# Low-rank part in four PSUM banks of its own, added by VectorE, with TensorE's work of a batch in blocks

## The chip, the cores and the metric

The kernel runs on one core of a Trainium2 chip. A core has TensorE (PE, matrix products), VectorE (DVE), ScalarE (ACT), GpSimd (POOL) and SyncE (SP), which here only issues DMAs. Each engine runs its own instruction list; semaphores order them. The metric is the device time of one execution in microseconds (us), taken as the median of several runs.

## The reference

There are 64 batches of x, each 128 channels by 2048 time steps, in fp32. Each batch b draws one of 16 square matrices W (128 by 128) and one of 64 low-rank adapters (B: 16 by 2048, A: 2048 by 16):

```python
    x = x + _L0_cond_ref(x, L0_cond_weights, itok_B_0_15)   # einsum('bct,bcd->bdt', x, W[cond])
    x = x + _L1_cond_ref(x, L1_cond_A, L1_cond_B, itok_B_4_50)
    # Bx = einsum('bni,bri->bnr', x, B[ids]);  out = einsum('bnr,bor->bno', Bx, A[ids])
    return x
```

With M = W + identity the first line is f = Mᵀx. The second adds the low-rank part: z = f · Bᵀ (a 16-vector for each channel), then A · z.

## The kernel before

A batch is held turned, time on the partitions: 16 chunks of 128 time steps, four chunks make a unit, and a unit of f fills one PSUM bank (128 by 512 fp32). There are 8 banks. For each batch:

- GpSimd picks M (`pick_m`, line 184) and splits A into a rounded part and a rest (`round_a`, `rest_of_a`, lines 188 and 193). VectorE turns 32 by 32 blocks of that (`turn_a`, line 290), GpSimd copies it to `at` (`place_at`, line 198).
- TensorE makes f unit by unit: `mix_unit`, line 349, four products of x (stationary) with M into `f_bank` or `f_last`.
- ScalarE copies each unit of f to SBUF, tile `ft` (`copy_unit`, line 249).
- TensorE sums z from `ft` and B: `sum_z`, line 362, 16 products whose stationary side is 16 columns wide, into one half of `zg_bank`. VectorE copies z (`join_z`, line 295), TensorE repeats it over the partitions (`spread_z`, line 372, into the other half of the same bank), VectorE splits it into g_hi and g_lo (`split_g`, lines 300 and 302).
- TensorE adds the low-rank part (`add_low_rank`, line 384): 32 products of 32 rows, accumulated onto f in the very banks that hold f. So f's banks stay taken from the mix to the end of the low rank.
- ScalarE copies units 3 and 1 to `x_out` and VectorE units 0 and 2 (`evacuate`, lines 253 and 283); SP stores `x_out` (line 157).

Units 0 to 2 of f have two banks each (for even and odd batches), unit 3 has one, `f_last`, for all batches; with `zg_bank` these are the eight. The order on each engine is written out by hand in the `turn` functions, four batches to a loop pass. On TensorE it interleaves: low rank of b; z of b+1 for three units; mix of unit 3 of b+1; mix of unit 0 of b+2; z of unit 3 of b+1; mix of unit 1; spread; mix of unit 2.

Of the kernel before, what the change touches and what calls it, by code (L numbers as in the profile page):

```python
# [11 lines left out]
P = 128  # L12
# [17 lines left out]
LEAVES = (3, 0, 1, 2)  # L30
BY_ACT, BY_DVE = LEAVES[0::2], LEAVES[1::2]
# [9 lines left out]
def exists(b, last):  # L41

    return not (last and b >= BODY)


def cond_lora_residual(nc, x, cond_ids, adapter_ids, weights, lora, out):
    with ExitStack() as ctx:  # L47
# [23 lines left out]
        ft = [[sbuf(f"ft{i}{u}", [P, UNIT]) for u in range(UNITS)] for i in range(2)]  # L71
# [36 lines left out]
        act_evacuated = sem("act_evacuated")  # L108
        dve_evacuated = sem("dve_evacuated")
# [7 lines left out]
        def _(sp):  # L117
# [26 lines left out]
            def turn(q, last):  # L144
                for k in range(BODY):
                    b = BODY * q + k
                    if not last:
                        sp.wait_ge(f_made, UNITS * (b + 1))
                        load_x(k, b + BODY)
                        adapter = adapter_of(b + BODY)  # L150
                        sp.wait_ge(z_done, b + 1)
                        sp.wait_ge(a_split, b + 1)
                        load_ab(k, adapter)
                    if not (last and k >= BODY - 2):
                        sp.wait_ge(act_evacuated, len(BY_ACT) * (b + 1))
                        sp.wait_ge(dve_evacuated, len(BY_DVE) * (b + 1))
                        sp.dma_start(out[b], x_out[k][:]).then_inc(stored[k], 16)
# [5 lines left out]
            for b in (BATCHES - 2, BATCHES - 1):  # L163
                for i, u in enumerate(LEAVES):
                    cols = slice(UNIT * u, UNIT * (u + 1))
                    if u in BY_ACT:
                        sp.wait_ge(act_evacuated, len(BY_ACT) * b + i // 2 + 1)
                    else:
                        sp.wait_ge(dve_evacuated, len(BY_DVE) * b + i // 2 + 1)
                    sp.dma_start(out[b, :, cols], x_out[b % BODY][:, cols]).then_inc(stored[b % BODY], 16)  # L170
# [4 lines left out]
        def _(pool):  # L175
# [29 lines left out]
            for k in range(2):  # L205
                pool.wait_ge(ab_loaded[k], 16)
                round_a(k)
                rest_of_a(k, k)
            pool.wait_ge(a_turned, 1)
            place_at(0)  # L210
# [3 lines left out]
            def turn(q, last):  # L214
                for k in range(BODY):
                    b = BODY * q + k
                    if exists(k + 3, last):
                        if live(UNITS * b):
                            pool.wait_ge(f_made, UNITS * b)
                        if exists(k + 2, last):  # L220
                            pool.wait_ge(a_turned, b + 1)
                            pool.wait_ge(ab_loaded[(k + 2) % BODY], 16 * (q + (k + 2) // BODY + 1))
                        pick_m((k + 3) % BODY, b + 3)
                    if exists(k + 2, last):
                        if not exists(k + 3, last):
                            pool.wait_ge(a_turned, b + 1)
                            pool.wait_ge(ab_loaded[(k + 2) % BODY], 16 * TURNS)
                        round_a((k + 2) % BODY)
                        pool.wait_ge(a_turned, b + 2)
                        if live(b):  # L230
                            pool.wait_ge(low_done, b)
                        rest_of_a((k + 2) % BODY, b + 2)
                        place_at(k + 1)
# [11 lines left out]
        def _(act):  # L245
            def copy_unit(k, u, b):

                act.wait_ge(f_made, UNITS * b + u + 1)
                nc.scalar.copy(ft[k % 2][u][:], f_bank[k % 2][u][:]).then_inc(copied, 1)  # L249

            def evacuate(k, u):

                nc.scalar.copy(x_out[k][:, UNIT * u:UNIT * (u + 1)], f_bank[k % 2][u][:]).then_inc(act_evacuated, 1)  # L253

            for u in range(UNITS):
                copy_unit(0, u, 0)
            for u in range(UNITS - 1):
                copy_unit(1, u, 1)

            def turn(q, last):  # L260
                for k in range(BODY):
                    b = BODY * q + k
                    if live(q):
                        act.wait_ge(stored[k], 16 * q)
                    act.wait_ge(low_done, b + 1)
                    for u in BY_ACT:
                        evacuate(k, u)
                    if exists(k + 1, last):
                        copy_unit(k + 1, UNITS - 1, b + 1)
                    if exists(k + 2, last):  # L270
                        for u in range(UNITS - 1):
                            copy_unit(k + 2, u, b + 2)

            turn(0, False)
            with act.Fori(1, TURNS - 1) as q:
                turn(q, False)
            turn(TURNS - 1, True)

        @block.vector
        def _(dve):  # L280
            def evacuate(k, u):

                nc.vector.tensor_copy(x_out[k][:, UNIT * u:UNIT * (u + 1)], f_bank[k % 2][u][:]).then_inc(dve_evacuated, 1)  # L283
# [26 lines left out]
            join_z(0)  # L310
            split_g(0)

            def turn(q, last):
                for k in range(BODY):
                    b = BODY * q + k
                    if live(q):
                        dve.wait_ge(stored[k], 16 * q)
                    dve.wait_ge(low_done, b + 1)
                    for u in BY_DVE:
                        evacuate(k, u)  # L320
                    if exists(k + 1, last):
                        turn_a(k + 1, b + 1)
                        join_z(b + 1)
                        split_g(b + 1)
# [7 lines left out]
        def _(pe):  # L332
            def mix_unit(k, u, b, turns):
# [8 lines left out]
                before = b - 1 if u == UNITS - 1 else b - 2  # L342
                if live(before + 1):
                    if u in BY_ACT:
                        pe.wait_ge(act_evacuated, len(BY_ACT) * before + BY_ACT.index(u) + 1)
                    else:
                        pe.wait_ge(dve_evacuated, len(BY_DVE) * before + BY_DVE.index(u) + 1)
                for c in range(IN_UNIT):
                    last = nc.tensor.matmul(f_bank[k % 2][u][:, P * c:P * (c + 1)],  # L349
# [4 lines left out]
            def sum_z(k, units, b, turns):  # L354

                if units[0] == 0:
                    pe.wait_ge(ab_loaded[k % BODY], 16 * turns)
                for u in units:
                    pe.wait_ge(copied, UNITS * b + u + 1)
                    for c in range(IN_UNIT):  # L360
                        first = RANK * (IN_UNIT * u + c)
                        last = nc.tensor.matmul(z_ps[TILE * c:TILE * c + RANK, :],  # L362
                                                ab_in[k % BODY][:, first:first + RANK],
                                                ft[k % 2][u][:, P * c:P * (c + 1)],
                                                start=(u == 0), stop=(u == UNITS - 1))
                if units[-1] == UNITS - 1:
                    last.then_inc(z_done, 1)
# [7 lines left out]
            def add_low_rank(k, b):  # L375

                pe.wait_ge(at_made, b + 1)
                for made, part in ((g_rounded, g_hi), (g_split, g_lo)):
                    pe.wait_ge(made, b + 1)
                    for c in range(IN_UNIT):  # L380
                        for u in range(UNITS):
                            rows = slice(BLOCK * u, BLOCK * (u + 1))
                            js = slice(c * (P // BLOCK), (c + 1) * (P // BLOCK))
                            last = nc.tensor.matmul(f_bank[k % 2][u][:, P * c:P * (c + 1)],  # L384
                                                    at[k % 2][rows, js, :].rearrange("m j i -> m (j i)"), part[rows, :],
                                                    start=False, stop=(part is g_lo and c == IN_UNIT - 1),
# [7 lines left out]
            mix_unit(1, 0, 1, 1)  # L394
            sum_z(0, (0, 1, 2, 3), 0, 1)
            mix_unit(1, 1, 1, 1)
            spread_z(0)
            mix_unit(1, 2, 1, 1)
# [61 lines left out]
```

## Time and profile before

| | |
|---|---|
| median of 3 runs | 427.61 us (427.53 to 429.12) |
| profiled execution, its own time | 432.05 us |
| profiled execution, span | 430.3 us |
| busy, share of the span: PE, PEld | 96%, 84% |
| busy: DVE, ACT, POOL | 42%, 51%, 31% |
| granted TensorE clock, mean | 0.991 of full speed |
| DMA | 152.37 MB, mean 354 GB/s |

PE are TensorE's matmuls, PEld its weight loads, which run beside matmuls. A busy PE doesn't mean PE at its peak: matmuls are pipelined, their ends are modelled, and the distance from one start to the next tells what a step costs. Each fp32 product is recorded twice, so 16 products are 32 records; the narrower low-rank products (fp32r) are recorded once.

### The profile page before, as it was taken

To read this page: it belongs to the slowest core of one execution; us is meant where nothing else is said; L and a number is where in the kernel's file an instruction comes from. 1 tells how busy PE (TensorE), PEld (TensorE's weight loads), DVE (VectorE), ACT (ScalarE), POOL (GpSimd) and SP (SyncE) were. 2 spreads that over 40 slices of the span, in tenths; PEclk is the share of its full clock that TensorE was granted. 3 is DMA by queue.
4 is the path that set the end of the run, shared out by engine and by line. 5 is a ranking of instruction groups with operands and counts; after the bars stand their busy time and mean duration, and the time that the engine had idled before them with its cause. 6 is when DMAs were issued, how large, how long until landed. Compare 5 with 4: busy or idle time off the path is not lost.

```text
span 430.3 us, 16398 instructions
## 1 busy us (share of the span) xinstructions
PE 412.4 (96%) x6272; PEld 363.2 (84%) x6272; DVE 179.2 (42%) x386; ACT 219.9 (51%) x385; POOL 131.9 (31%) x263
## 2 busy tenths in 40 slices
PE   2999998999999999999999999999999999999993
PEld 2988886888888888888888888888888888888882
DVE  1334433444344344344344444444434434434433
ACT  1455553455555555555555555555555555555551
POOL 1343231332332331332332332233233133233220
PEclk9999998999999999999999999999999999999998
DMA  7999997899999999999999999999999999999645
GB/s 234 340 404 422 403 377 308 312 375 361 372 383 358 366 382 360 357 393 367 362 380 368 360 379 373 366 363 383 360 359 393 360 364 381 358 363 389 258 178 195
DMA packets 29777, 152.37 MB, mean 354 GB/s; under 512 B 3268, under 2 KB 3524, under 8 KB 13764
## 3 DMA queue, kind: packets, MB, share of 16 engines
q1 hardware_dynamic: 29764, 152.19, 95.2%
q8 instruction: 9, 0.15, 0.1%
q14 instruction: 4, 0.03, 0.0%
HBM read 85.07 MB, written 67.11 MB: 354 GB/s over the span
## 4 chain that ended last, share of the span: by engine, by line
PE 96%; DMA 1%; issue 1%; SPq 1%; DVE 0%; DVEq 0%; ACT 0%; POOL 0%; POOLq 0%
PE f_bank L349 44%; PE zg_bank L362 17%; PE f_last L349 17%; PE f_bank L384 15%; PE zg_bank L372 3%; DMA w_first<-in_L_cond_weights 1%; PE f_last L384 0%; SPq L131 0%; DVE x_out L283 0%; SPq L134 0%; DVEq L47 0%; ACT ft L249 0%; POOL m_sel L204 0%; SPq L127 0%; DVE z_t L295 0%
## 5 line engine op out<-in xcount | busy, mean ns | idle before, releaser
L349 PE MATMUL f_bank<-m_sel,x_in 128*128 128x128 f32 x1536 | 212.3, 282 | 8.2 <-POOL m_sel L204 8.2
L349 PEld LDWEIGHTS f_bank<-m_sel,x_in 128*128 128x128 f32 x1536 | 189.7, 195 | 21.7 <-issue 21.7
L249 ACT COPY ft<-f_bank 128x512 f32<-128x512 f32 x192 | 112.4, 586 | 118.2 <-PE f_bank L349 118.2
L193 POOL TENSOR_TENSOR a_hl<-ab_in,a_hl 128x256 fp32r<-128x256 f32 x64 | 46.6, 728 | 258.4 <-DVE at_turn L290 258.1
L283 DVE COPY x_out<-f_bank 128x512 f32<-128x512 f32 x128 | 82.4, 686 | 88.3 <-PE f_last L384 88.3
L362 PE MATMUL zg_bank<-ft,ab_in 128*16 128x128 f32 x2048 | 80.8, 276 | 0.7 <-ACT ft L249 0.7
L349 PEld LDWEIGHTS f_last<-m_sel,x_in 128*128 128x128 f32 x512 | 62.3, 192 | 17.2 <-ACT x_out L253 15.0
L349 PE MATMUL f_last<-m_sel,x_in 128*128 128x128 f32 x512 | 74.7, 289 | 2.1 <-issue 2.1
L249 ACT COPY ft<-f_last 128x512 f32<-128x512 f32 x64 | 37.5, 585 | 51.3 <-PE f_last L349 51.3
L362 PEld LDWEIGHTS zg_bank<-ft,ab_in 128*16 128x16 f32 x2048 | 44.8, 96 | 13.1 <-ACT ft L249 0.9
L253 ACT COPY x_out<-f_last 128x512 f32<-128x512 f32 x64 | 37.5, 585 | 35.3 <-PE f_last L384 35.3
L295 DVE COPY z_t<-zg_bank 128x128 f32<-128x128 f32 x64 | 18.6, 291 | 80.2 <-PE zg_bank L362 80.2
L290 DVE STREAM_TRANSPOSE at_turn<-a_hl 128x512 f32<-128x512 f32 x64 | 44.9, 701 | 11.3 <-POOL a_hl L193 11.3
L300 DVE CAST g_hi<-zg_bank 128x128 fp32r<-128x128 f32 x64 | 18.6, 291 | 63.1 <-PE zg_bank L372 63.1
L384 PE MATMUL f_bank<-g_hi,at 32*128 32x128 f32 x768 | 42.5, 283 | 0.5 <-DVE g_hi L300 0.5
L384 PE MATMUL f_last<-g_hi,at 32*128 32x128 f32 x256 | 42.1, 283 | 0.0
L198 POOL CAST at<-at_turn 128x512 fp32r<-128x512 f32 x64 | 39.0, 610 | 5.1 <-DVE at_turn L290 5.1
L384 PEld LDWEIGHTS f_bank<-g_hi,at 32*128 32x128 f32 x768 | 33.5, 185 | 8.2 <-issue 0.6
L384 PE MATMUL f_bank<-g_lo,at 32*128 32x128 f32 x768 | 39.2, 270 | 0.0
L384 PE MATMUL f_last<-g_lo,at 32*128 32x128 f32 x256 | 38.8, 270 | 0.0
L253 ACT COPY x_out<-f_bank 128x512 f32<-128x512 f32 x64 | 37.9, 592 | 0.0
L384 PEld LDWEIGHTS f_bank<-g_lo,at 32*128 32x128 f32 x768 | 33.9, 187 | 0.0
(18 smaller groups left out, 187.2 us busy)
## 6 DMA issues: line engine op xcount, KB each, us to landing
x_in<-in_x SPq DMA_DIRECT2D x63, 1024.0 KB, 7.0
out<-x_out SPq DMA_DIRECT2D x62, 1024.0 KB, 5.0
ab_in<-in_lora SPq DMA_DIRECT2D x64, 256.0 KB, 5.8
out<-x_out SPq DMA_DIRECT2D x8, 256.0 KB, 3.2
x_in<-in_x SPq DMA_DIRECT2D x4, 256.0 KB, 4.0
w_first<-in_L_cond_weights SPq DMA_DIRECT2D x2, 64.0 KB, 4.2
ids<-in_itok_B SPq DMA_DIRECT2D x2, 0.2 KB
w_all<-in_L_cond_weights SPq DMA_DIRECT2D x1, 0.5 KB, 8.6
```

The lines of the kernel that those rows point to most:

```text
L193: nc.gpsimd.tensor_tensor(a_hl[k % 2][:, :, RANK:HL], raw_a(k), a_hl[k % 2][:, :, 0:RANK], ALU.subtract).then_inc(a_split, 1)
L198: nc.gpsimd.tensor_copy(at[k % 2][:], at_turn[:]).then_inc(at_made, 1)
L249: nc.scalar.copy(ft[k % 2][u][:], f_bank[k % 2][u][:]).then_inc(copied, 1)
L253: nc.scalar.copy(x_out[k][:, UNIT * u:UNIT * (u + 1)], f_bank[k % 2][u][:]).then_inc(act_evacuated, 1)
L283: nc.vector.tensor_copy(x_out[k][:, UNIT * u:UNIT * (u + 1)], f_bank[k % 2][u][:]).then_inc(dve_evacuated, 1)
L290: nc.vector.transpose(at_turn[:], a_hl[k % 2][:].bitcast(F32)).then_inc(a_turned, 1)
L295: nc.vector.tensor_copy(z_t[:], z_ps).then_inc(z_joined, 1)
L300: nc.vector.tensor_copy(g_hi[:], g_ps).then_inc(g_rounded, 1)
L349: last = nc.tensor.matmul(f_bank[k % 2][u][:, P * c:P * (c + 1)], x_in[k][:, UNIT * u + P * c:UNIT * u + P * (c + 1)], m_sel[k][:], start= ...
L362: last = nc.tensor.matmul(z_ps[TILE * c:TILE * c + RANK, :], ab_in[k % BODY][:, first:first + RANK], ft[k % 2][u][:, P * c:P * (c + 1)], s ...
L372: nc.tensor.matmul(g_ps, spread[:].rearrange("k n r -> k (n r)"), z_t[:], start=True, stop=True).then_inc(g_done, 1)
L384: last = nc.tensor.matmul(f_bank[k % 2][u][:, P * c:P * (c + 1)], at[k % 2][rows, js, :].rearrange("m j i -> m (j i)"), part[rows, :], sta ...
```

## The change

The low-rank part no longer accumulates onto f. It has four banks of its own, `low_bank`, and f gets three, `f_bank0` to `f_bank2`; unit 3 goes to bank 0 again (`BANK_OF`). ScalarE copies f to `ft` and does nothing else; `ft` has four buffers, one for each batch of a pass. VectorE writes all of `x_out`: x_out = low_bank + ft, four adds a batch. TensorE does a batch's work in blocks, and the low rank comes one batch later. SP issues the A and B load and the store later against the x load; GpSimd does A one batch ahead in place of two.

```diff
-LEAVES = (3, 0, 1, 2)
-BY_ACT, BY_DVE = LEAVES[0::2], LEAVES[1::2]
+BANK_OF = (0, 1, 2, 0)
...
-        ft = [[sbuf(f"ft{i}{u}", [P, UNIT]) for u in range(UNITS)] for i in range(2)]
+        ft = [[sbuf(f"ft{i}{u}", [P, UNIT]) for u in range(UNITS)] for i in range(BODY)]
...
-        f_last = psum("f_last")
-        f_bank = [[psum(f"f_bank{i}{u}") for u in range(UNITS - 1)] + [f_last] for i in range(2)]
+        f_bank = [psum(f"f_bank{i}") for i in range(max(BANK_OF) + 1)]
+        low_bank = [psum(f"low_bank{u}") for u in range(UNITS)]
... SP, in turn(q, last)
-                        adapter = adapter_of(b + BODY)
-                        sp.wait_ge(z_done, b + 1)
-                        sp.wait_ge(a_split, b + 1)
-                        load_ab(k, adapter)
-                    if not (last and k >= BODY - 2):
-                        sp.wait_ge(act_evacuated, len(BY_ACT) * (b + 1))
-                        sp.wait_ge(dve_evacuated, len(BY_DVE) * (b + 1))
-                        sp.dma_start(out[b], x_out[k][:]).then_inc(stored[k], 16)
+                    if begun(b - 1) and exists(k + BODY - 1, last):
+                        adapter = adapter_of(b + BODY - 1)
+                        sp.wait_ge(z_done, b)
+                        sp.wait_ge(a_split, b)
+                        load_ab((k - 1) % BODY, adapter)
+                    if begun(b - 2):
+                        sp.wait_ge(added, UNITS * (b - 1))
+                        sp.dma_start(out[b - 2], x_out[(k - 2) % BODY][:]).then_inc(stored[(k - 2) % BODY], 16)
... ScalarE
+                    if live(q):
+                        act.wait_ge(added, UNITS * (b - BODY + 1))
+                    for u in range(UNITS):
+                        copy_unit(k, u, b)
... VectorE
+            def add_unit(k, u):
+
+                nc.vector.tensor_tensor(x_out[k][:, UNIT * u:UNIT * (u + 1)], low_bank[u][:], ft[k][u][:],
+                                        ALU.add).then_inc(added, 1)
+
+            def add_batch(k, b, turns):
+
+                if live(turns):
+                    dve.wait_ge(stored[k], 16 * turns)
+                dve.wait_ge(low_done, b + 1)
+                for u in range(UNITS):
+                    add_unit(k, u)
... TensorE
-                before = b - 1 if u == UNITS - 1 else b - 2
+                left = UNITS * (b if u == UNITS - 1 else b - 1) + (1 if u == UNITS - 1 else UNITS if u == 0 else u + 1)
+                if live(left):
+                    pe.wait_ge(copied, left)
...
+            def sum_z(k, b, turns):
+
+                pe.wait_ge(ab_loaded[k], 16 * turns)
+                pe.wait_ge(copied, UNITS * (b + 1))
+                if live(b):
+                    pe.wait_ge(g_split, b)
...
             def add_low_rank(k, b):
 
                 pe.wait_ge(at_made, b + 1)
+                if live(b):
+                    pe.wait_ge(added, UNITS * b)
...
-                            last = nc.tensor.matmul(f_bank[k % 2][u][:, P * c:P * (c + 1)],
+                            last = nc.tensor.matmul(low_bank[u][:, P * c:P * (c + 1)],
...
+                        for u in range(UNITS):
+                            mix_unit(k + 1, u, b + 1, q + (k + 1) // BODY + 1)
+                    sum_z(k, b, q + 1)
+                    if begun(b - 1):
+                        add_low_rank((k - 1) % BODY, b - 1)
+                    spread_z(b)
```

TensorE, one batch of the kernel before, in the first pass of four batches, with the low rank's last rows ahead of it (zg_bank is written by z with ft and ab_in, and by the spread with z_t):

```order
L384 MATMUL f_bank<-g_lo,at 128x128 x3
L384 MATMUL f_last<-g_lo,at 128x128
L362 MATMUL zg_bank<-ft,ab_in 16x128 x12
L349 MATMUL f_last<-m_sel,x_in 128x128 x4
L349 MATMUL f_bank<-m_sel,x_in 128x128 x4
L362 MATMUL zg_bank<-ft,ab_in 16x128 x4
L349 MATMUL f_bank<-m_sel,x_in 128x128 x4
L372 MATMUL zg_bank<-z_t,spread 128x128
L349 MATMUL f_bank<-m_sel,x_in 128x128 x4
L384 MATMUL f_bank<-g_hi,at 128x128 x3
```

TensorE, one batch of the changed kernel, in the first pass, with the spread ahead of it (the low rank is that of the batch before; f's units 0 and 3 share a bank):

```order
L354 MATMUL zg_bank<-z_t,spread 128x128
L331 MATMUL f_bank<-m_sel,x_in 128x128 x16
L345 MATMUL zg_bank<-ft,ab_in 16x128 x16
L368 MATMUL low_bank<-g_hi,at 128x128 x16
L368 MATMUL low_bank<-g_lo,at 128x128 x16
L354 MATMUL zg_bank<-z_t,spread 128x128
```

The four mixes have moved together, z is in one piece behind them, and the low rank stands between z and the spread.

VectorE, one batch of the first pass before:

```order
L283 COPY x_out<-f_bank 128x512 x2
L290 STREAM_TRANSPOSE at_turn<-a_hl 128x512
L295 COPY z_t<-zg_bank 128x128
L300 CAST g_hi<-zg_bank 128x128
L302 TENSOR_TENSOR g_lo<-zg_bank,g_hi 128x128
```

VectorE, one batch of the changed first pass (x_out and the adds are those of the batch before, z_t and g_hi of this one):

```order
L283 COPY z_t<-zg_bank 128x128
L262 TENSOR_TENSOR x_out<-low_bank,ft 128x512 x4
L288 CAST g_hi<-zg_bank 128x128
L290 TENSOR_TENSOR g_lo<-zg_bank,g_hi 128x128
L278 STREAM_TRANSPOSE at_turn<-a_hl 128x512
```

Four adds now stand between z_t and g_hi, where the two stood next to each other with two copies behind the split.

## Rows read from the trace of the kernel before

**Rows 1.** The page: busy time and share of each engine; the chain that ended last.

```profile
PE 412.4 (96%) x6272; PEld 363.2 (84%) x6272; DVE 179.2 (42%) x386; ACT 219.9 (51%) x385; POOL 131.9 (31%) x263
...
PE 96%; DMA 1%; issue 1%; SPq 1%; DVE 0%; DVEq 0%; ACT 0%; POOL 0%; POOLq 0%
```

**Rows 2.** Timeline, weight loads of a batch: start, length, engine, line, tiles, count [idle before].

```profile
200.77 0.19 PEld L384 LDWEIGHTS f_bank<-g_hi,at 32*128 32x128 f32 x3
...
201.81 0.57 PEld L362 LDWEIGHTS zg_bank<-ft,ab_in 128*16 128x16 f32 x24
...
202.59 0.97 PEld L349 LDWEIGHTS f_last<-m_sel,x_in 128*128 128x128 f32 x8 [0.21 <-ACT x_out L253]
...
203.48 0.97 PEld L349 LDWEIGHTS f_bank<-m_sel,x_in 128*128 128x128 f32 x8
...
204.57 0.13 PEld L362 LDWEIGHTS zg_bank<-ft,ab_in 128*16 128x16 f32 x8
...
204.92 0.97 PEld L349 LDWEIGHTS f_bank<-m_sel,x_in 128*128 128x128 f32 x8 [0.21 <-issue]
...
205.80 0.30 PEld L372 LDWEIGHTS zg_bank<-z_t,spread 128*128 128x128 f32 x2
...
206.03 0.97 PEld L349 LDWEIGHTS f_bank<-m_sel,x_in 128*128 128x128 f32 x8
...
207.12 0.19 PEld L384 LDWEIGHTS f_bank<-g_hi,at 32*128 32x128 f32 x3
```

**Rows 3.** Timeline at the start: z of batch 0, its z_t, M of batch 2.

```profile
15.18 0.79 PEld L362 LDWEIGHTS zg_bank<-ft,ab_in 128*16 128x16 f32 x32
...
16.18 0.97 PEld L349 LDWEIGHTS f_bank<-m_sel,x_in 128*128 128x128 f32 x8 [0.21 <-issue]
...
16.31 0.29 DVE L295 COPY z_t<-zg_bank 128x128 f32<-128x128 f32 x1 [1.73 <-PE zg_bank L362]
...
18.13 0.46 POOL L184 TENSOR_TENSOR m_sel<-w_all,ident 128x128 f32<-128x128 f32 x1 [2.59 <-DMA w_all<-in_L_cond_weights]
```

**Rows 4.** Timeline of VectorE in the same batch.

```profile
199.98 0.29 DVE L300 CAST g_hi<-zg_bank 128x128 fp32r<-128x128 f32 x1 [0.99 <-PE zg_bank L372]
200.31 0.29 DVE L302 TENSOR_TENSOR g_lo<-zg_bank,g_hi 128x128 fp32r<-128x128 f32 x1
201.93 1.29 DVE L283 COPY x_out<-f_bank 128x512 f32<-128x512 f32 x2 [1.33 <-PE f_last L384]
203.14 0.70 DVE L290 STREAM_TRANSPOSE at_turn<-a_hl 128x512 f32<-128x512 f32 x1
```

**Rows 5.** The page, DMA issues: KB each, us from issue to landing.

```profile
x_in<-in_x SPq DMA_DIRECT2D x63, 1024.0 KB, 7.0
```

**Rows 6.** Stretches: length, busy us (instructions) by engine, PEclk, DMA share, GB/s.

```profile
30.00:40.00 10.00, 10.00 (x171) 8.86 (x170) 4.76 (x11) 5.66 (x10) 2.04 (x4) 1.00 1.01 419
40.00:50.00 10.00, 10.00 (x136) 8.93 (x135) 4.17 (x10) 5.17 (x9) 4.16 (x8) 1.00 1.02 413
...
100.00:150.00 50.00, 50.00 (x760) 43.97 (x752) 22.10 (x48) 26.75 (x48) 16.38 (x32) 1.00 1.01 370
```

**Rows 7.** Timeline at the end: last z_t, spread, g_hi, low rank, copies.

```profile
421.88 0.29 DVE L295 COPY z_t<-zg_bank 128x128 f32<-128x128 f32 x1 [1.03 <-PE zg_bank L362]
422.23 0.30 PEld L372 LDWEIGHTS zg_bank<-z_t,spread 128*128 128x128 f32 x2 [0.70 <-DVE z_t L295]
...
422.75 0.29 DVE L300 CAST g_hi<-zg_bank 128x128 fp32r<-128x128 f32 x1 [0.58 <-PE zg_bank L372]
...
423.16 0.22 PEld L384 LDWEIGHTS f_bank<-g_hi,at 32*128 32x128 f32 x3 [0.64 <-issue]
...
424.42 1.29 DVE L283 COPY x_out<-f_bank 128x512 f32<-128x512 f32 x2 [1.05 <-PE f_last L384]
```

**Rows 8.** Timeline: the spreads on either side of the longest batch.

```profile
61.61 0.30 PEld L372 LDWEIGHTS zg_bank<-z_t,spread 128*128 128x128 f32 x2
...
71.85 0.30 PEld L372 LDWEIGHTS zg_bank<-z_t,spread 128*128 128x128 f32 x2
```

More of the change, by code:

```diff
@@ L38, in live, with exists, begun @@
     return not (isinstance(count, int) and count <= 0)
-def exists(b, last):
-    return not (last and b >= BODY)
+def exists(k, last):
+    return not (last and k >= BODY)
+def begun(b):
+    return not (isinstance(b, int) and b < 0)
 def cond_lora_residual(nc, x, cond_ids, adapter_ids, weights, lora, out):
@@ L204, in _ @@
                 nc.gpsimd.tensor_tensor(m_sel[k][:], w_first[k][:], ident[:], ALU.add).then_inc(m_picked, 1)
[L205 to L210, printed above, removed]
+            pool.wait_ge(ab_loaded[0], 16)
+            round_a(0)
+            rest_of_a(0, 0)
             pool.wait_ge(w_in, 16)
@@ L248, in copy_unit @@
                 act.wait_ge(f_made, UNITS * b + u + 1)
[L249 to L258, printed above, removed]
+                nc.scalar.copy(ft[k][u][:], f_bank[BANK_OF[u]][:]).then_inc(copied, 1)
             def turn(q, last):
@@ L263, in turn @@
                     if live(q):
[L264 to L272, printed above, removed]
+                        act.wait_ge(added, UNITS * (b - BODY + 1))
+                    for u in range(UNITS):
+                        copy_unit(k, u, b)
             turn(0, False)
-            with act.Fori(1, TURNS - 1) as q:
+            with act.Fori(1, TURNS) as q:
                 turn(q, False)
-            turn(TURNS - 1, True)
         @block.vector
         def _(dve):
-            def evacuate(k, u):
-                nc.vector.tensor_copy(x_out[k][:, UNIT * u:UNIT * (u + 1)], f_bank[k % 2][u][:]).then_inc(dve_evacuated, 1)
+            def add_unit(k, u):
[7 more added lines that the diff above has]
+                    add_unit(k, u)
             def turn_a(k, b):
@@ L352, in mix_unit @@
                 last.then_inc(f_made, 1)
[L354 to L359, printed above, removed]
+            def sum_z(k, b, turns):
+                pe.wait_ge(ab_loaded[k], 16 * turns)
+                pe.wait_ge(copied, UNITS * (b + 1))
+                if live(b):
+                    pe.wait_ge(g_split, b)
+                for u in range(UNITS):
                     for c in range(IN_UNIT):
@@ L383, in add_low_rank @@
                             js = slice(c * (P // BLOCK), (c + 1) * (P // BLOCK))
-                            last = nc.tensor.matmul(f_bank[k % 2][u][:, P * c:P * (c + 1)],
+                            last = nc.tensor.matmul(low_bank[u][:, P * c:P * (c + 1)],
                                                     at[k % 2][rows, js, :].rearrange("m j i -> m (j i)"), part[rows, :],
-                                                    start=False, stop=(part is g_lo and c == IN_UNIT - 1),
+                                                    start=(part is g_hi and c == 0), stop=(part is g_lo and c == IN_UNIT - 1),
                                                     skip_group_check=True)
```

84 lines of the change are left out of this document (27 added, 57 removed).

## The prediction, made before the changed kernel was run

> **What bounds the kernel now.** I read the page's engine shares and its chain first [rows 1]: TensorE is busy for 96% of the span and is 96% of the chain that ended last; VectorE is busy for 42%, ScalarE 51%, GpSimd 31%. So only what TensorE spends or waits for counts, and I need its batch in pieces. Since matmuls overlap, I read the starts of the weight loads (PEld), one start to the next.
>
> One batch, from low rank to low rank, is 207.12 − 200.77 = 6.35 us; most are 0.04 longer, with the wait on x_out behind z at 0.25; 6.38 on average. Its pieces [rows 2]:
> - low rank, 32 loads: 201.81 − 200.77 = 1.04
> - z of three units, 24 loads: 202.59 − 201.81 = 0.78
> - mix of f_last (8 loads: each fp32 matmul appears twice): 0.89
> - mix of a unit, with z behind it: 204.57 − 203.48 = 1.09
> - z of the fourth unit, 8 loads: 0.35
> - mix, with the spread behind it: 0.88
> - spread: 0.23
> - mix, with the low rank behind it: 1.09
>
> Two things stand in this list. First, 8 loads of a mix take 0.89 where another full-array product follows and 1.09 where z or the low rank follows: 0.20 for changing kind. The same step lies behind z: between its last load and the first of the mix PEld is idle for 0.21, once put down to ScalarE and once to "issue", with nothing to wait for. At the start 32 z loads in one piece take 16.18 − 15.18 = 1.00 [rows 3], while 24 and 8 apart take 0.78 + 0.35 = 1.13. So a change of kind costs about 0.2 at either side, waits or not. Second, two mixes in a row cost nothing extra although the second one's unit has its own wait: waits that are met are free.
>
> There are five such changes in a batch now: low to z, z to mix, mix to z, z to mix, mix to low.
>
> **The change on TensorE.** The same 98 matmul records a batch (6272 / 64 [rows 1]), in another order: four mixes, z, low rank of the batch before, spread. Three changes of kind are left: mix to z, z to low, low to spread.
> - mixes: 3 × 0.89 + 1.09 = 3.76 (before 0.89 + 1.09 + 0.88 + 1.09 = 3.95)
> - z in one block: 1.00 (before 1.13)
> - low rank: 1.04, spread: 0.23 as before
> - sum 6.03, against 6.38: 0.35 less in each batch.
>
> Two of these changes, z to low and low to spread, are not in the trace. From below each could cost nothing (0.4 less a batch), from above twice the 0.2 that others cost (0.4 more). Four that it does show cost 0.20 to 0.21, in both directions between full-array and narrow products; the fifth, low to z, narrow to narrow, lies inside the 1.04. I take the same for the two new ones: they are inside the 1.00 and the 1.04.
>
> **What the new waits ask for.** I count from T, the load of a batch's spread, which follows the low rank of the batch before.
> - VectorE starts its x_out work about 0.17 behind T: 201.93 against 201.81 here [rows 2, 4], up to 0.19 in other batches. Two 512-wide copies and the start of the next instruction are 203.14 − 201.93 = 1.21, so 0.605 each. The adds are four tensor_tensor from PSUM and SBUF. No such 512-wide row exists. From below: the copy's 0.605. From above: four times the 128-wide tensor_tensor out of PSUM, g_lo's 4 × 0.29 = 1.16 [rows 4]. I take 0.605, for g_lo takes the same 0.29 as the g_hi cast of the same width, so the second operand adds nothing there. Four adds: 2.42.
> - g_hi 0.33 and g_lo 0.29 behind them: done at T + 0.17 + 2.42 + 0.62 = T + 3.21, seen by TensorE at about T + 3.35.
> - The next z waits for g_split (it shares zg_bank), and would start at T + 0.23 + 3.76 = T + 3.99. The wait is met with 0.6 to spare. It comes out late once an add takes over 0.76.
> - turn_a (0.70) ends at T + 3.95, before z is done at T + 5.0; then z_t takes 0.29, and the spread is due at T + 6.03. Met. Queued behind join_z on VectorE are the adds, which can't start before T + 6.2 anyway.
> - GpSimd works 131.9 / 64 = 2.1 us a batch [rows 1] between a turn_a and the next; its at copy is due about 6 us after it is done. Met.
> - ScalarE has four copies instead of six: 219.9 / 385 = 0.57 each, 2.3 of 6.03. f_bank0 is filled twice a batch: the fourth mix starts 2.67 after the first, whose bank is filled 1.2 after its first load and copied 0.6 later. Met.
> - The DMA queue (SP) now waits for added of the batch two back, between the loads. x of batch b + 4 is issued when mix b is done and is needed 4 × 6.03 − 3.76 = 20 us later; a load lands in 7.0 [rows 5]. Stores have as much room. Met.
>
> **Transfers.** A batch moves 2.36 MB (two of 1 MB, one of 256 KB), 370 GB/s at 6.38. At 6.03 it is 391. Between 30 and 50 us the queue, with a backlog from the start, moved 419 and 413 GB/s [rows 6] with stores among the loads, so the floor of a batch is about 2.36 / 0.416 = 5.7 us. The 370 of the later stretch is what the kernel asks for; the DMA share of 1.00 stands beside both rates and tells nothing apart.
>
> By the Trainium skill ("DMA: Bandwidth & Descriptors", section "Where 436 GB/s comes from") transfers between HBM and SBUF are bound at about 358 GB/s per core; an estimate by it puts 152 MB at 426 us, no gain at all. The trace disagrees: 419 GB/s over 10 us, and 370 for hundreds. It is a rival below by its rows, though.
>
> **Start.** The mix of batch 1 starts as now, one mix ahead of z(0): 15.18 − 1.09 = 14.09 [rows 3]. z(0) then starts 3.76 later, at 17.85; its z_t starts 16.31 − 15.18 = 1.13 behind that, and the spread has to wait for it, as at the end of the kernel now, where it is loaded 422.23 − 421.88 = 0.35 behind z_t's start [rows 7]. T of batch 0 is 19.3. m_sel of batch 2 is picked at 18.13 + 0.46 [rows 3] and mix 2 starts at 19.5; the x load behind w_all may come up to 1 us later, which no row tells.
>
> **Loop.** 62 turns with a mix: 62 × 6.03 = 373.9. In one batch now (61.61 to 71.85, 10.24 instead of 6.38 [rows 8]) the engines stood still in the loop's second pass. The new loop has the same passes, so I keep the 3.9. T of batch 62 is 19.3 + 373.9 + 3.9 = 397.1.
>
> **End.** No mixes cover the last batch: z(63) waits for g_split, T + 3.5; z to 4.5; low rank of 62 to 5.54; its adds start at 5.7 and take 2.42; g_hi starts at 8.13 and the low rank of 63 follows 0.41 behind (423.16 − 422.75 now [rows 7]) at 8.54; adds start 1.26 later (424.42 − 423.16) at 9.8; the last of four ends 3 × 0.605 + 0.69 later, T + 12.3. Now 4.6 us lie between the last copy's end, 424.42 + 1.29, and the end of the span at 430.3, some 0.6 of it stores queued behind one another; with adds spaced by 0.6, 4.0 are left. End of span: 397.1 + 16.3 = 413.4.
>
> The profiled execution has a span of 430.3 and a time of 432.05; so 16.9 less. The median of the runs is 427.61, 4.4 below the profiled time. Taking the same 16.9 off the median gives **410.7 us**, 4% faster.
>
> **Rivals.**
> 1. *The transfers bind.* If 370 GB/s were the rate of a long mix of loads and stores, not the demand, the batch stays at 6.38 and the longer end eats the rest: 427 to 430. For it: the share of 1.00, and the burst at 419 that lies in a stretch with more loads. Against it: no wait of TensorE on a load anywhere but at the start, and a landing time of 7 us that doesn't grow. A rate of 385 would give 6.13 and 62 × 0.10 = 6 more: 417. Chance 0.10, half for each.
> 2. *The adds become the bound: slower.* Place: VectorE, between the low rank and g_split. The loop is 0.17 + 4a + 0.62 + 0.15, then z 1.00 and low 1.04, so 2.98 + 4a, with a the time of an add. It decides above a = 0.76, and is slower than now above a = 0.85. Price, if GpSimd's 2.1 us of work a batch all held the adds up (they read SBUF, the copies didn't): 2.98 + 2.42 + 2.1 = 7.5, and 62 × 1.1 = 69 more than now, 497; at a = 1.16 it is 505. Against it: g_lo's second operand comes from SBUF as well and it takes 0.29 like the copy. Chance 0.06. By the Trainium skill ("SBUF — State Buffer", section "Who interferes with whom") a VectorE instruction with at most one SBUF input doesn't contend with GpSimd, so the price would be nothing; the g_lo row agrees, but GpSimd was mostly idle beside it.
> 3. *The new changes of kind cost more* than the five shown, 0.1 each: 6.23, 12 more, 423. Chance 0.05. If they cost nothing, the transfers' floor of 5.7 and the adds' 5.4 come next: 62 × 0.3 less, 392. Chance 0.04.
>
> The forecast has 0.75; its own range is 407 to 415 (the stall of 3.9 gone, or 1 us at the start and a few at the end more). The range for 8 in 10 takes in the milder transfer case: 405 to 419. What a measurement of this kernel can tell from no change is 0.5%, 2.1 us: faster 0.88, within 0.05 (half of rival 1), slower 0.07.
>
> **What would show it.** Right: PEld starts 3.76 from the first mix to z, 1.00, 1.04 and 0.23 in every batch; adds of about 0.69, 0.6 apart; z waiting for nothing; 390 GB/s. Wrong: PEld idle before z, released by g_lo (rival 2); PE waiting on x_in, or x_in landing in 15 us and more (rival 1); over 0.3 us between the last z load and the first of the low rank (rival 3).

## The result and the profile after

| | before | after |
|---|---|---|
| median | 428.37 us (4 runs, 427.53 to 431.22) | 414.32 us (4 runs, 414.18 to 414.51) |
| profiled execution: time, span | 432.05, 430.3 | 414.18, 412.1 |
| busy, share of the span: PE, PEld | 96%, 84% | 95%, 88% |
| DMA, mean | 354 GB/s | 370 GB/s |

The ratio is 0.9661 (95% interval 0.9613 to 0.9709): 3.4% faster. The forecast was 410.7 with a range of 405 to 419.

The page, shares and chain, to be held against [rows 1]:

```profile
PE 391.6 (95%) x6272; PEld 364.7 (88%) x6272; DVE 249.7 (61%) x514; ACT 151.6 (37%) x257; POOL 134.0 (33%) x263
...
PE 95%; DVE 2%; DMA 1%; SPq 1%; issue 0%; DVEq 0%; ACT 0%; POOL 0%; POOLq 0%
```

TensorE is still the chain. VectorE's busy share has gone from 42% to 61% and ScalarE's from 51% to 37%. VectorE has come into the chain with 2%, which is the end of the kernel.

The next reading is the batch, as in [rows 2]: the starts of the weight loads, now for the changed kernel (line 345 is z, 368 the low rank, 354 the spread, 331 the mixes).

```profile
200.44 0.53 PEld L368 LDWEIGHTS low_bank<-g_hi,at 32*128 32x128 f32 x16 [0.21 <-issue]
...
200.88 0.53 PEld L368 LDWEIGHTS low_bank<-g_lo,at 32*128 32x128 f32 x16
...
201.49 0.30 PEld L354 LDWEIGHTS zg_bank<-z_t,spread 128*128 128x128 f32 x2
...
201.71 3.65 PEld L331 LDWEIGHTS f_bank<-m_sel,x_in 128*128 128x128 f32 x32
...
205.48 0.79 PEld L345 LDWEIGHTS zg_bank<-ft,ab_in 128*16 128x16 f32 x32
...
206.48 0.53 PEld L368 LDWEIGHTS low_bank<-g_hi,at 32*128 32x128 f32 x16 [0.21 <-issue]
```

Low rank 201.49 − 200.44 = 1.05, spread 0.22, four mixes 205.48 − 201.71 = 3.77, z 1.00: 6.04 from low rank to low rank, and 6.03 or 6.04 in all batches of the loop but one. The prediction had 1.04, 0.23, 3.76, 1.00. Both new changes of kind can be read here: PEld stands idle for 0.21 between z and the low rank, and the second half of the low rank, with the spread behind it, takes 201.49 − 200.88 = 0.61 where the first half takes 0.44, so low rank to spread costs 0.17.

VectorE in the same stretch, to be held against [rows 4], with one GpSimd row:

```profile
200.58 0.29 DVE L283 COPY z_t<-zg_bank 128x128 f32<-128x128 f32 x1 [1.31 <-PE zg_bank L345]
...
201.68 2.48 DVE L262 TENSOR_TENSOR x_out<-low_bank,ft 128x512 f32<-128x512 f32 x4 [0.81 <-PE low_bank L368]
...
204.08 0.28 DVE L288 CAST g_hi<-zg_bank 128x128 fp32r<-128x128 f32 x1
...
204.40 0.29 DVE L290 TENSOR_TENSOR g_lo<-zg_bank,g_hi 128x128 fp32r<-128x128 f32 x1
204.61 0.70 DVE L278 STREAM_TRANSPOSE at_turn<-a_hl 128x512 f32<-128x512 f32 x1
...
207.72 2.48 DVE L262 TENSOR_TENSOR x_out<-low_bank,ft 128x512 f32<-128x512 f32 x4 [0.81 <-PE low_bank L368]
207.73 0.40 POOL L187 CAST a_hl<-ab_in 128x256 fp32r<-128x256 f32 x1
```

Four adds take 2.48 from the first start to the last end (three pitches and 0.68, so 0.60 each), g_hi starts 2.40 behind the first, and g_lo ends at 204.69. The z that waits for it is loaded at 205.48, 0.79 later, with no wait shown. The adds at 207.72 have a GpSimd copy of 0.40 beside their start and take the same 2.48.

The transfers, first a load's way to landing, then a long stretch (columns as in [rows 5, 6]):

```profile
x_in<-in_x SPq DMA_DIRECT2D x63, 1024.0 KB, 8.7
```

```profile
100.00:150.00 50.00, 50.00 (x802) 46.77 (x802) 32.78 (x68) 19.87 (x34) 16.67 (x32) 1.00 1.01 393
```

The rate is 393 GB/s instead of 370, and a load lands after 8.7 us instead of 7.0. With 20 us of room that is hidden.

The start: weight loads up to the first spread.

```profile
8.01 5.96 PEld L331 LDWEIGHTS f_bank<-m_sel,x_in 128*128 128x128 f32 x32 [8.01 <-issue]
...
14.90 3.65 PEld L331 LDWEIGHTS f_bank<-m_sel,x_in 128*128 128x128 f32 x32 [0.93 <-issue]
...
18.67 0.79 PEld L345 LDWEIGHTS zg_bank<-ft,ab_in 128*16 128x16 f32 x32
...
20.15 0.30 PEld L354 LDWEIGHTS zg_bank<-z_t,spread 128*128 128x128 f32 x2 [0.70 <-DVE z_t L283]
```

The end: TensorE's last z and low ranks and VectorE's last adds, then the granted clock of that stretch.

```profile
397.87 0.85 PEld L345 LDWEIGHTS zg_bank<-ft,ab_in 128*16 128x16 f32 x32 [3.02 <-issue]
...
399.13 0.93 PEld L368 LDWEIGHTS low_bank<-g_hi,at 32*128 32x128 f32 x16 [0.41 <-POOL at L197]
...
401.03 0.50 PEld L354 LDWEIGHTS zg_bank<-z_t,spread 128*128 128x128 f32 x2
...
401.23 2.48 DVE L262 TENSOR_TENSOR x_out<-low_bank,ft 128x512 f32<-128x512 f32 x4 [1.69 <-PE low_bank L368]
...
404.02 0.96 PEld L368 LDWEIGHTS low_bank<-g_hi,at 32*128 32x128 f32 x16 [2.49 <-issue]
...
406.15 2.48 DVE L262 TENSOR_TENSOR x_out<-low_bank,ft 128x512 f32<-128x512 f32 x4 [1.92 <-PE low_bank L368]
```

```profile
400.00:412.00 12.00, 3.81 (x58) 3.23 (x54) 5.45 (x10) 0.00 (x0) 0.00 (x0) 0.50 0.58 194
```

From these the span can be taken apart. Before: first spread at 17.06, last but one at 416.39, end 430.3; after: 20.15, 394.56, 412.1. In one batch each kernel lost time, 3.85 and 0.35 us. Without that the 62 batches between the two spreads take 395.5 before and 374.1 after, 21.4 less; the start costs 3.1 more, and the end 17.5 instead of 13.9, 3.6 more. 21.4 − 3.1 − 3.6 = 14.7, and the medians differ by 14.05.

### The profile page after: what moved, and what is told of

The parts are those of the page before. It is cut to its first block, busy times and chain, and to the rows that moved or that the text cites. A ratio compares the mean times of both kernels' runs of the same rounds, so it can differ in the third digit from the quotient of the medians.

```text
span 412.1 us, 16202 instructions
## 1 busy us (share of the span) xinstructions
PE 391.6 (95%) x6272; PEld 364.7 (88%) x6272; DVE 249.7 (61%) x514; ACT 151.6 (37%) x257; POOL 134.0 (33%) x263
## 4 chain that ended last, share of the span: by engine, by line
PE 95%; DVE 2%; DMA 1%; SPq 1%; issue 0%; DVEq 0%; ACT 0%; POOL 0%; POOLq 0%
PE f_bank L331 56%; PE low_bank L368 17%; PE zg_bank L345 16%; PE zg_bank L354 6%; DVE x_out L262 2%; DMA w_first<-in_L_cond_weights 1%; SPq L133 0%; SPq L136 0%; ACT ft L244 0%; DVEq L51 0%; POOL m_sel L203 0%; DVE g_hi L288 0%; SPq L129 0%; DVE g_lo L290 0%; DVE z_t L283 0%
## 5 line engine op out<-in xcount | busy, mean ns | idle before, releaser
L331 PE MATMUL f_bank<-m_sel,x_in 128*128 128x128 f32 x2048 | 241.9, 277 | 8.9 <-POOL m_sel L203 8.0
L331 PEld LDWEIGHTS f_bank<-m_sel,x_in 128*128 128x128 f32 x2048 | 236.2, 194 | 9.2 <-issue 9.2
L244 ACT COPY ft<-f_bank 128x512 f32<-128x512 f32 x256 | 150.3, 587 | 240.9 <-PE f_bank L331 235.3
L262 DVE TENSOR_TENSOR x_out<-low_bank,ft 128x512 f32<-128x512 f32 x256 | 158.8, 682 | 53.4 <-PE low_bank L368 53.4
L368 PEld LDWEIGHTS low_bank<-g_hi,at 32*128 32x128 f32 x1024 | 34.5, 189 | 16.0 <-issue 15.4
L368 PE MATMUL low_bank<-g_hi,at 32*128 32x128 f32 x1024 | 43.7, 288 | 2.2 <-DVE g_hi L288 2.2
L368 PE MATMUL low_bank<-g_lo,at 32*128 32x128 f32 x1024 | 40.4, 275 | 0.0
L183 POOL TENSOR_TENSOR m_sel<-w_all,ident 128x128 f32<-128x128 f32 x62 | 28.2, 456 | 22.4 <-issue 18.3
L368 PEld LDWEIGHTS low_bank<-g_lo,at 32*128 32x128 f32 x1024 | 35.0, 191 | 0.0
L354 PE MATMUL zg_bank<-z_t,spread 128*128 128x128 f32 x128 | 31.6, 329 | 0.4 <-DVE z_t L283 0.4
```

Source lines behind the costliest of these rows:

```text
L183: nc.gpsimd.tensor_tensor(m_sel[k][:], w_all[:, cond, :], ident[:], ALU.add).then_inc(m_picked, 1)
L244: nc.scalar.copy(ft[k][u][:], f_bank[BANK_OF[u]][:]).then_inc(copied, 1)
L262: nc.vector.tensor_tensor(x_out[k][:, UNIT * u:UNIT * (u + 1)], low_bank[u][:], ft[k][u][:], ALU.add).then_inc(added, 1)
L331: last = nc.tensor.matmul(f_bank[BANK_OF[u]][:, P * c:P * (c + 1)], x_in[k][:, UNIT * u + P * c:UNIT * u + P * (c + 1)], m_sel[k][:], star ...
L354: nc.tensor.matmul(g_ps, spread[:].rearrange("k n r -> k (n r)"), z_t[:], start=True, stop=True).then_inc(g_done, 1)
L368: last = nc.tensor.matmul(low_bank[u][:, P * c:P * (c + 1)], at[k % 2][rows, js, :].rearrange("m j i -> m (j i)"), part[rows, :], start=(p ...
```

## The experiments

**The stall.** The kernel before, profiled again.

> The kernel before, unchanged, profiled a second time. Question: is the stall of 3.9 us in one batch of the second loop pass part of the kernel or of one execution? Theory A (of one execution): no batch longer than 6.5 us except the first and last, a span of about 426.5, and a profiled time of about 428. Theory B (of the kernel, as the prediction had it): one batch of about 10 us again at about 62 us, span 430.

Measured: 429.29 us, span 427.5. The spreads on either side of the longest batch, and the loads around the idle time in it:

```profile
60.89 0.30 PEld L372 LDWEIGHTS zg_bank<-z_t,spread 128*128 128x128 f32 x2
...
66.40 0.41 PEld L349 LDWEIGHTS f_last<-m_sel,x_in 128*128 128x128 f32 x3 [1.70 <-issue]
...
69.05 0.30 PEld L372 LDWEIGHTS zg_bank<-z_t,spread 128*128 128x128 f32 x2
```

The batch takes 8.16 instead of 6.39, so 1.8 us are lost, in the same batch of the second loop pass as in [rows 8], where it was 3.9. Of the kernels below, the one with z in one block lost 0.45 there and the one with the split low rank nothing; the changed kernel lost 0.35, and in its second profile nothing. Neither theory holds as put: the place belongs to the loop, the length to the execution. The first trace shows where its larger loss comes from:

```profile
67.67 0.71 PEld L349 LDWEIGHTS f_last<-m_sel,x_in 128*128 128x128 f32 x3 [2.25 <-issue]
68.26 1.83 PEld L349 LDWEIGHTS f_bank<-m_sel,x_in 128*128 128x128 f32 x8
```

```profile
68.00:70.00 2.00, 2.00 (x11) 2.00 (x10) 0.00 (x0) 0.58 (x1) 0.75 (x2) 0.50 0.85 299
```

There PEld stood idle for 2.25 us, and behind that the granted clock was 0.50, the lower level of 1.2 GHz: eight loads of a mix took 1.83 instead of 0.97. In the second profile PEld stood idle for 1.70, and the granted clock stayed at 1.00. So 0.55 of the 2.1 between the two losses is idle time, and most of the other 1.5 goes with work at the lower clock.

**Is it the changes of kind?** The changed kernel with the spread between the low rank's halves:

```diff
                     if begun(b - 1):
-                        add_low_rank((k - 1) % BODY, b - 1)
+                        add_low_rank((k - 1) % BODY, b - 1, (0,))           # the g_hi half
                     spread_z(b)
+                    if begun(b - 1):
+                        add_low_rank((k - 1) % BODY, b - 1, (1,))           # the g_lo half
```

> The changed kernel with the spread put between the g_hi half and the g_lo half of the low rank: the same instructions, two more changes of kind a batch (low to spread, spread to low, low to mix in place of low to spread). Theory (each change of kind costs TensorE 0.2 us): batch 6.03 + 0.4 = 6.44, span 412 + 25 = 437, with no new wait before z. Rival (changes of kind are not what was saved; it was the waits on the copies out of the f banks and the work taken from ScalarE): batch stays 6.03 to 6.1, span 412 to 416.

Measured: 437.95 us, span 435.9, batch 6.38 (one in four 6.46, which stays unexplained). Weight loads of a batch (369 is the low rank):

```profile
203.06 0.79 PEld L345 LDWEIGHTS zg_bank<-ft,ab_in 128*16 128x16 f32 x32
...
204.05 0.53 PEld L369 LDWEIGHTS low_bank<-g_hi,at 32*128 32x128 f32 x16 [0.21 <-issue]
...
204.65 0.30 PEld L354 LDWEIGHTS zg_bank<-z_t,spread 128*128 128x128 f32 x2
...
205.07 0.53 PEld L369 LDWEIGHTS low_bank<-g_lo,at 32*128 32x128 f32 x16
...
205.67 2.42 PEld L331 LDWEIGHTS f_bank<-m_sel,x_in 128*128 128x128 f32 x21
```

The two halves take 0.60 each, together 0.15 more than in one piece, and the spread 0.42 instead of 0.22. The instructions are the same and z still waits for nothing, yet the batch is 0.35 longer, of the expected 0.40: the whole gain of a batch is undone by two changes of kind, at 0.15 and 0.20. The rival's 412 to 416 is out.

**Is the order alone enough?** The kernel before, its banks and copies kept:

```diff
-                        sum_z(k + 1, (0, 1, 2), b + 1, q + (k + 1) // BODY + 1)
                         mix_unit(k + 1, 3, b + 1, q + (k + 1) // BODY + 1)
                     if exists(k + 2, last):
                         mix_unit(k + 2, 0, b + 2, q + (k + 2) // BODY + 1)
                     if exists(k + 1, last):
-                        sum_z(k + 1, (3,), b + 1, q + (k + 1) // BODY + 1)
+                        sum_z(k + 1, (0, 1, 2, 3), b + 1, q + (k + 1) // BODY + 1)
```

> The kernel before with its banks and copies as they are; only TensorE's order differs: low rank, mix of unit 3, mix of unit 0, z of all four units in one block, mix, spread, mix. One change of kind fewer and z in one piece (0.33 less), but the mix of unit 3 stands right behind the low rank and has to wait until f_last is copied out. Theory (the blocks need the low rank to have banks of its own): f_last is loaded 0.78 behind the low rank's end as now, batch = 1.04 + 0.78 + 0.89 + 1.09 + 1.00 + 0.88 + 0.23 + 1.09 = 7.00, span about 430 + 62 x 0.62 = 465. Rival (the order alone brings the gain, banks don't matter): batch about 6.1, span about 410.

Measured: 468.74 us, span 467.0, batch 6.99 to 7.05. The mix of f_last and the z behind the next mix:

```profile
203.15 0.97 PEld L349 LDWEIGHTS f_last<-m_sel,x_in 128*128 128x128 f32 x8 [0.89 <-ACT x_out L253]
...
205.13 0.79 PEld L362 LDWEIGHTS zg_bank<-ft,ab_in 128*16 128x16 f32 x32
```

The batch was forecast at 7.00. The mix stands idle for 0.89 until ScalarE has copied f_last out. Fewer changes of kind are worth nothing while the low rank holds f's banks: the banks are what allows the order.

**The floor of the transfers.** SP alone works; its loop in outline (no x_out is computed, the tiles hold zeros):

```diff
+                    sp.wait_ge(x_loaded[k], 16 * (q + 1))
+                    sp.wait_ge(ab_loaded[k], 16 * (q + 1))
+                        load_x(k, b + BODY)
+                        load_ab(k, adapter_of(b + BODY))
+                        sp.wait_ge(stored[k], 16 * q)
+                    sp.dma_start(out[b], x_out[k][:]).then_inc(stored[k], 16)
```

> Only the transfers of the kernel: the same loads of x, of A and B and of the matrices, and stores of as many bytes from tiles filled with zeros (nothing is computed), four deep in each direction. Theory (the floor of a batch is 2.36 MB at about 416 GB/s = 5.7 us, below TensorE's 6.03): rate 400 to 420 GB/s, span 370 to 385. Rival (a long mix of loads and stores moves at about 390 GB/s, so the changed kernel already stands at the transfers' limit): 385 to 392 GB/s, span 392 to 400. By the 358 GB/s of the Trainium skill's page DMA: Bandwidth & Descriptors it would be 426.

Measured: 369.39 us, span 367.6. Two stretches, and a load's landing (the busy columns here are VectorE and GpSimd):

```profile
50.00:100.00 50.00, 0.00 (x0) 0.00 (x0) 1.00 1.02 424
...
300.00:350.00 50.00, 0.00 (x0) 0.00 (x0) 1.00 1.02 425
```

```profile
x_in<-in_x SPq DMA_DIRECT2D x63, 1024.0 KB, 21.0
```

A lasting mix of loads and stores moves 425 GB/s: 2.36 / 0.425 = 5.55 us a batch. The changed kernel's 6.03 stands 0.48 above it; the rival's 385 to 392 is out. When the transfers do bind, a landing takes 21 us; 8.7 is what it takes when they don't. The DMA share is 1.00 to 1.02 in both. The Trainium skill ("DMA: Bandwidth & Descriptors", section "Where 436 GB/s comes from") has transfers between HBM and SBUF bound at about 358 GB/s per core. For this core, the only one that the program runs on, that doesn't hold: the measurement decides.

**How far VectorE is from the path.** One and two more 512-wide copies ahead of the adds:

```diff
                 dve.wait_ge(low_done, b + 1)
+                for i in range(n):         # n = 1, n = 2
+                    nc.vector.tensor_copy(idle_out[:], low_bank[i][:]).then_inc(idled, 1)
                 for u in range(UNITS):
```

> The changed kernel with one more 512-wide VectorE copy (low_bank to a tile that nobody reads) ahead of each batch's four adds. Theory (z waits for g_split only once VectorE is over 0.64 us later than now: g_lo ends 3.20 behind the spread's load, z is loaded at 3.99, and needs 0.12 behind g_lo): the copy's 0.605 just fits, batch 6.03 to 6.06, span 412 to 414. Rival (VectorE is already on the path): 0.6 more a batch, span 449.

> The changed kernel with two such copies ahead of the adds. Theory: 1.21 more on VectorE, 0.65 of it hidden, so z is loaded at 3.20 + 1.21 + 0.12 = 4.53 behind the spread, batch 6.03 + 0.55 = 6.58, span 412 + 34 = 446. Rival (the wait costs more than the lateness, since a late z also makes z_t, the spread and the adds late): over 7.0 a batch, span over 470.

Measured with one copy: 417.65 us, batch 6.03, unchanged. Its span of 415.6 lies above the expected 412 to 414 and 3.5 above the changed kernel's: 2.4 at the end, where nothing covers the copy, 0.7 ahead of the first spread, where no copy runs yet, and 0.4 in the long batch of the second pass (0.8 lost instead of 0.35). With two copies: 451.99 us, span 450.0, batch 6.58. Rows of the second (358 is the spread, 294 g_lo, 349 z):

```profile
197.85 0.30 PEld L358 LDWEIGHTS zg_bank<-z_t,spread 128*128 128x128 f32 x2
...
201.95 0.29 DVE L294 TENSOR_TENSOR g_lo<-zg_bank,g_hi 128x128 fp32r<-128x128 f32 x1
...
202.36 0.81 PEld L349 LDWEIGHTS zg_bank<-ft,ab_in 128*16 128x16 f32 x32 [0.64 <-issue]
```

g_lo ends at 202.24 and z is loaded 0.12 later, 4.51 behind the spread; forecast were 4.53 and a batch of 6.58. So the step "z waits once VectorE is 0.6 late" holds to a few hundredths, and in the loop a late z costs its lateness and no more. The span missed its forecast of 446 by 4, all of it at the end: 21.7 behind the last but one spread instead of the changed kernel's 17.5.

**The two ends.** The changed kernel again as the measure, and with its ends redone (in outline):

```diff
+            return low_bank[3] if isinstance(b, int) and b == 0 and u == 3 else f_bank[BANK_OF[u]]
+                    if first:                  # TensorE, batch 0, ahead of its spread
+                        mix_unit(2, 0, 2, 1)
...
+            if isinstance(b, int) and b == BATCHES - 2:      # banks of the last low ranks
+                return (f_bank + [low_bank[0]])[u]
+            if isinstance(b, int) and b == BATCHES - 1:
+                return (low_bank[1:] + [zg_bank])[u]
...
+                        split_g(b)             # VectorE, the last two batches
+                        add_batch(k - 1, b - 1, q, (0, 1))
+                        join_z(b + 1)
+                        add_batch(k - 1, b - 1, q, (2, 3))
+                        split_g(b + 1)
```

> The changed kernel unchanged, timed beside the others. Theory: span 412, time 414, ratio 0.966; every batch 6.03 but one in the second loop pass, which is up to a few us longer and differs from execution to execution.

> The changed kernel with other work at its two ends and the same loop. Start: unit 3 of batch 0 goes to a low bank, so that the mix of batch 1 need not wait for its copy (0.8), and the first mix of batch 2 stands ahead of the first spread, whose z_t is late (0.5). End: the low rank of batches 62 and 63 goes to banks that are free by then (f_bank, zg_bank), and VectorE does the splits of 62 and 63 ahead of the adds that stand before them. Theory (no mix covers VectorE's adds in the last two batches, 17.5 us from the last but one spread to the end): the last add ends about 9.5 behind that spread in place of 14.1, span 412.1 - 0.8 - 0.5 - 4.6 = 406, time 408, 1.4% under the changed kernel. Rival (the end is set by the stores, 3 MB at about 425 GB/s, or by TensorE's half clock after its idle time): 1 us or less from the end, span 410.

Measured: 414.0 us (413.84 to 414.21; ratio to the kernel before 0.9655, 0.9592 to 0.9717) and 410.85 us (410.66 to 412.39; 0.9578, 0.9516 to 0.964). The ranges of the two don't meet; about half of the forecast 5.9 us came. The profiled execution was the slowest of the four. In it the last add ended 9.4 behind the last but one spread, as expected (395.45; 404.85), but the span only 15.0 behind it. SP's stores, and two stretches:

```profile
400.69 5.72 SPq L179 DMA_DIRECT2D out<-x_out  x8
```

```profile
395.00:400.00 5.00, 3.47 (x88) 2.76 (x84) 4.24 (x11) 0.00 (x0) 0.62 (x1) 1.00 0.08 30
...
402.00:404.00 2.00, 0.00 (x0) 0.00 (x0) 2.00 (x4) 0.00 (x0) 0.00 (x0) 0.50 0.94 352
```

Almost nothing moves for 5 us (30 GB/s), and then three batches' stores run at once, here at 352 GB/s: the adds had been the bound, and behind them the stores are. That is the expectation's rival, in part. The gain at the start didn't come in this execution: PEld waited 1.49 ahead of the mix of batch 1 and 1.40 ahead of the first mix of batch 2, both put down to x by the profile, and x of batch 2 stands behind the 1 MB of all the matrices in the queue.

**The loads' order, and TensorE's first mixes.**

```diff
+            load_w_first(0); load_w_first(1); load_x(1, 1); load_ab(0, ...)     # SP; 64 KB each w_first
+            load_x(2, 2); load_ab(1, ...); load_w_first(2); load_x(3, 3); load_w_first(3); ...
+            sp.dma_start(w_all[:], ...)        # now the last
...
-            for b in (BATCHES - 2, BATCHES - 1):
+            for b in (BATCHES - 3, BATCHES - 2, BATCHES - 1):                    # stored unit by unit
... and, in the second kernel alone, on TensorE ahead of the first mix
+            for _ in range(20):
+                nc.tensor.matmul(low_bank[0][:, 0:P], ident[:], ident[:], start=True, stop=True)
```

> As e8_both_ends, and further: the 1 MB load of all sixteen matrices is issued last instead of ahead of the x of batches 2 and 3, whose matrices are loaded one by one (64 KB each), and the output of batch 61 is stored unit by unit. Theory (the start is set by the transfers, TensorE waits for x behind the matrices; at the end three batches of stores are bunched, since no transfer runs in the 5 us before): the first mixes still run at half clock, mix 1 starts at about 14.1, the second spread about 1 us earlier than in e8, the end 1.5 earlier; time 408. Rival (the stores at the end move at their rate whatever starts them): no gain at the end, 410.

> As e9_loads_first, with twenty products of the identity with itself on TensorE in the 7 us before the first mix, in which it waits for the first matrix (they are extra work; nobody reads them). Theory (the first 32 loads take 5.95 us because the granted clock is at its lower level, 1.2 GHz, after the idle start): the first mixes take 3.6 us, mix 1 starts at about 12.5 if its x has landed, 1.5 to 2 us less than e9: time 406. Rival (mix 1 waits for x or its matrix anyway): the same time as e9.

Measured: 407.72 us (407.38 to 408.89; ratio 0.949, 0.9432 to 0.9549) and 407.83 us (406.75 to 408.38; 0.9476, 0.9417 to 0.9536). The first met its forecast of 408: its span ends 13.6 behind the last but one spread instead of 15.0, close to the 1.5 expected from stores that start earlier, and the rest of the gain is at the start. The second missed its 406. Weight loads of the two at the start, and a stretch of the first (granted clock in the third column from the end):

```profile
8.02 4.27 PEld L367 LDWEIGHTS f_bank<-m_sel,x_in 128*128 128x128 f32 x24 [8.02 <-issue]
...
13.10 3.65 PEld L367 LDWEIGHTS f_bank<-m_sel,x_in 128*128 128x128 f32 x32
...
18.75 0.30 PEld L390 LDWEIGHTS zg_bank<-z_t,spread 128*128 128x128 f32 x2
```

```profile
5.00:10.00 5.00, 1.95 (x9) 1.99 (x10) 0.00 (x0) 0.00 (x0) 0.84 (x2) 1.00 0.90 312
```

```profile
1.56 6.39 PEld L417 LDWEIGHTS low_bank<-ident 128*128 128x128 f32 x40 [1.56 <-POOL ident L193]
8.29 2.75 PEld L367 LDWEIGHTS f_bank<-m_sel,x_in 128*128 128x128 f32 x24 [0.34 <-issue]
...
13.01 3.65 PEld L367 LDWEIGHTS f_bank<-m_sel,x_in 128*128 128x128 f32 x32 [1.07 <-DMA x_in<-in_x]
```

With work ahead of them the first 24 loads take 2.75 instead of 4.27, one in 0.11 as in the loop. So the idle start does make the first loads slower, about 0.20 each at first (ten in the 1.99 us of the stretch). That the clock is the reason, as the expectations have it, is not shown: the granted clock reads 1.00 in that stretch, where it read 0.50 beside the slow loads of the stall above. The faster first mixes gain nothing, since the next mix now waits 1.07 for x ("DMA x_in") and starts at 13.01 against 13.10. The rival holds there. The two versions can't be told apart and are the fastest at hand, 5% under the kernel before, and 6 us under the changed kernel, which was timed in other rounds.

## Why the prediction was right, and where its sizes were off

**The batch.** 6.38 → 6.03 was forecast and measured. The step that carried it, a change of kind costs 0.2 us and five become three, was confirmed by putting two back (0.15 and 0.20). That z to low and low to spread cost what the others do was a choice between bounds 0.4 apart on either side; the trace after shows 0.21 and 0.17.

**VectorE.** An add at 0.605, chosen by the copy's row, measured 0.60. g_lo's end was put at T + 3.21 and came at T + 3.20, z at T + 3.99 and came there. The slower rival (adds held up by GpSimd) didn't appear. The adds with a GpSimd copy of 0.40 beside them took 2.48 as well, as the Trainium skill has it ("SBUF — State Buffer", section "Who interferes with whom").

**The transfers.** The floor was forecast at 5.7 from 20 us with a backlog, and measured at 5.55. The transfers are hidden, as forecast.

**The start, mis-sized by 0.85.** The step "the mix of batch 1 starts as now, at 14.09" failed: it started at 14.90. Units 3 and 0 share bank 0, so this mix waits for ScalarE's copy of the unit just made. In the loop z and the low rank stand between; ahead of the first z nothing does. The diff showed it, and I had counted this wait for the fourth mix only. x of batch 2 was not late, which the prediction left open.

**The end, mis-sized by 1.2.** The steps came in the order forecast. z(63) was early, 3.3 behind the last but one spread instead of 3.5 (the prediction's own sum for g_lo gives 3.35), and the low rank of 62 had a wait that the prediction lacks, for GpSimd's at (0.41 by its row), which took that back. What cost the time: TensorE idled for 3.0 us ahead of z(63) and for 2.5 ahead of the last low rank, and the granted clock fell to its lower level, 1.2 GHz (0.50 in the row of 400 to 412). The low rank took 401.03 − 399.13 = 1.90 where I had 1.04 by the loop's rows, and the adds behind the last one started 406.15 − 404.02 = 2.13 behind it where I had 1.26. A duration from a dense loop isn't that of the same work behind an idle stretch. Against it, the last store came 3.5 behind the last add, not 4.0.

**The stall, mis-sized by 3.5.** I kept 3.9 in the new kernel's loop; it was 0.35, and 1.8 in the old kernel's second profile. That the span came within 1.3 (413.4 forecast, 412.1 measured) is in part luck: this error more than hides the two before it, which go the other way (413.4 − 3.55 + 0.85 + 1.2 + 0.2 = 412.1, the 0.2 being the loop). In the median it drops out, for the 16.9 taken off has a stall of 3.9 on both sides. There the two ends show: the medians fell by 14.05, 2.85 less than forecast, and 2.1 of that are the ends; 0.2 is the loop (374.1 instead of 373.9), 0.3 the time around the span (2.1 us after, 1.75 before), and the small rest isn't told apart. The other 0.8 of the 3.6 between 410.7 and 414.3 is the base: the median before was 427.61 in three runs when the forecast was made and 428.37 with a fourth.

**The rivals' prices.** Rival 1 put a kernel that stays at 6.38 at 427 to 430. By the prediction's own terms it is 410.7 + 62 × 0.35 = 432, since the start and the end are longer by 2.2 and 2.4. The 497 and 505 of rival 2 leave the same 4.6 out. Neither changes what was chosen.

## What to carry to other kernels

Where matmuls of different shapes alternate and TensorE is the bound, count the changes of kind, not only the matmuls, and lay a batch out so that each kind comes once; check first whether a shared accumulation bank forces the alternation. An order that leans on a batch's mixes to cover another engine has no cover in the last batches: look at the first and last batch of such a pipeline by themselves, with durations at the clock they will have. Take a stall that shows in one profile out of both sides before two spans are compared, or a forecast span can come out near for a wrong reason, as here.

## What the runs showed of the hardware

- A change between full-array, 16-column and 32-row products cost TensorE 0.15 to 0.21 us each time, waits or not; a second mix behind a mix cost nothing beyond its own 0.89.
- A VectorE tensor_tensor of 512 fp32 out of PSUM and SBUF was recorded at 0.68, but four in a row stood 0.60 apart, like copies.
- From the end of VectorE's g_lo to the weight load that waited for it: 0.12 us (two copies ahead of the adds).
- Loads and stores together, four of each in flight and nothing else at work: 425 GB/s over 300 us, with 21 us from issue to landing.
- Behind TensorE's idle 2.25 us in the longer stall, and at the end with idle times of 3.0 and 2.5 us in it, the granted clock was 0.50 (68 to 70 us before; 400 to 412 us after). Behind the idle start it reads 1.00, though the first loads take 0.20 each.
- In the second pass of the loop six of eleven profiles lost time in one batch, the loop being the old or the changed one: 3.9 and 1.8 us in the two of the kernel before, 0.35 to 0.8 in four others, nothing in five. What makes it was not tested and stays open.
